# A gate and a normalisation moved from VectorE to GpSimd, w3 in quarters, and six smaller moves in a two-layer kernel

## The chip, the cores and the metric

One core of a Trainium2 chip. The metric is the device time of one execution in microseconds (us); the times of three executions and one profiled execution are given below. Engines: TensorE (PE, its weight loads PEld), VectorE (DVE), ScalarE (ACT), GpSimd (POOL), and SyncE (SP), which issues most transfers (SPq).

## What is computed

Two transformer layers over 16 sequences of 512 tokens, width 128, all in fp32. Layer 0: an attention with a running state and a gated dense network. Layer 1, cut to what matters here:

```python
x = x + attn0(norm(x)) + ffn0(norm(x))       # ffn0: ... gelu(h2 . gelu(h1 . h)) then w3
xn = layernorm(x)
# gated linear attention ("GLA"), 4 heads
gk = log_sigmoid(xn @ gk_w1 @ gk_w2 + gk_b2) / 16
o  = gated_linear_scan(xn @ Wq, xn @ Wk, xn @ Wv, gk)
o  = o / sqrt(mean(o * o) + eps) * g_norm
g  = xn @ Wg
r1 = x + (o * g * sigmoid(g)) @ Wo
# 16-head softmax attention, head width 8, then a layer norm and a routed dense network
a  = softmax(q @ k.T / sqrt(8)) @ v
y  = layernorm(xn + a @ Wo + bo)
expert = floor(y @ router_w + router_b) mod 4
out = r1 + layernorm(y + relu(y @ W1[expert] + b1) @ W2[expert] + b2)
```

## The kernel before, in words

The program has three stages, each a block in which every engine has its own list of instructions; they meet through semaphores that only count up.

**Layer 0** (`layer0_sequences`) runs a pipeline over the 16 sequences. SP also prepares weights for layer 1 there: in three of its rounds (`stage "W"`) it loads 12 chunks (L295), ScalarE and VectorE split each into a high and a low part (L443, L509), and SP stores them (L298). One buffer serves all chunks. Ahead of the load of chunk 4, SP issues 12 plain copies into the table of expert weights (`table_parts`, L292). `pad` (L300) writes 2 MB of padding rows in each round.

**Layer 1** (`attention`) is a pipeline over rounds -4 to 16; in a full round (0 to 12) each of nine stages works on another sequence. `OUT_OF` says which: F0 and F (the last product of layer 0's dense network, h2 and w3) are 4 and 3 sequences ahead, A0 (layer norm, transpose, projections of q and k) 2, A1 and B (GLA; row maxima of the scores) 1, C (softmax and product with v) 0, and C2 (output projection, norm, router, scatter) one behind. A round has 32 steps. `attention_order` writes one list of (stage, kind, number) by step with `put(step, stage, kind, number)`, and every engine walks this list in order and does its own part of each entry. In each step p TensorE makes scores p (L1305), ScalarE the exponentials (L1425); TensorE makes score rows for the maxima (L1287) and VectorE reduces them (L1578); the score rows have one pair of banks, so TensorE's maxima of step p wait for VectorE's reduction of step p-1. In odd steps TensorE multiplies with v (L1315). What else a step holds, of what is touched:

- step 12, `front`: VectorE's statistics of x1; GpSimd's `root` (L1662 adds eps, L1664 takes the power -0.5). Step 14, `front2`: VectorE's four `tensor_scalar` make xn (L1477). Step 16: TensorE transposes xn (L1194), GpSimd adds a bias row (L1676).
- step 13, `U`: VectorE makes three states from a bank of TensorE's; the second and third are updates of the one before (L1545); GpSimd then makes h_blk (L1685). Step 14, `A`: TensorE's products (L1237) take the bank of U, so they wait for the states. VectorE multiplies them with the causal mask (L1550).
- step 21: tanh of the gate on ScalarE; VectorE copies the outputs O. Step 24: `osquare` (ScalarE), `gate` (VectorE, L1516: (tanh + 1) * g), `O2` (VectorE's reduction L1559 and L1562, then GpSimd's power L1698). Step 25: `O3` (VectorE L1565, then GpSimd's product with the gate, L1702), and `rank` (TensorE). Step 26: `slot` (VectorE, L1640 to L1648, with the product L1644). Steps 24 and 26: the two halves of w3 (L1186); step 27: `x1` (VectorE adds, L1485; SP stores). Steps 28 and 29: transposes of o. Step 31: the GLA output product and the scatter.
- `warm`: in rounds -2, -1 and 13 to 15 TensorE makes five idle products (L1166) in each even step (`live`, `few`).

TensorE's first instruction of the stage waits for all dense weights (`f_loaded`, 2 MB, issued in a small block before the stage). In round -2 the first sequence is normed, transposed, projected and stored by 24 transfers (L1096), then loaded in the layout of the row maxima (L1106).

**Experts** (`experts`): VectorE first turns the counts into a plan of 19 groups of 512 tokens (L1879 to L1909), for which SP waits; then each group goes through two products; VectorE norms and `write`s it (L1945) after GpSimd's `root` (L1971, L1974), and GpSimd scatters it by four indirect transfers (L1983). GpSimd's list is root(k+1), then the scatters of k.

## Time and profile before

| | us |
|---|---|
| median of three executions | 2771.05 (2768.88 to 2776.47) |
| profiled execution, its time | 2765.3 |
| its span, first to last instruction | 2763.5 |
| layer 0 stage / layer 1 stage / experts stage, from about | 0 / 977 / 2597 |
| mean granted TensorE clock | 0.949 |

The granted clock is 1.0 at TensorE's full level and 0.5 at half. In the timeline each row has the start, the duration, the engine, the line, the operation, output and inputs, their shapes, the number of merged instructions, and in brackets how long the engine had been idle and who ended that. The views by source give the number of instructions, the least, median and greatest duration in ns, and the stretch in which they lie. In the windows each row has the stretch, its length, the busy us and instructions of PE, PEld, DVE, ACT and POOL, the mean granted clock, the DMA share and GB/s; where it is of one line alone, only the busy us and instructions of its engine.

### The profile page before, as it was taken

To read this page: it belongs to the slowest core of one execution; us is meant where nothing else is said; L and a number is where in the kernel's file an instruction comes from. 1 tells how busy PE (TensorE), PEld (TensorE's weight loads), DVE (VectorE), ACT (ScalarE), POOL (GpSimd) and SP (SyncE) were. 2 spreads that over 40 slices of the span, in tenths; PEclk is the share of its full clock that TensorE was granted. 3 is DMA by queue.
4 is the path that set the end of the run, shared out by engine and by line. 5 is a ranking of instruction groups with operands and counts; after the bars stand their busy time and mean duration, and the time that the engine had idled before them with its cause. 6 is when DMAs were issued, how large, how long until landed. Compare 5 with 4: busy or idle time off the path is not lost. (4 is left out here: it accounts for less than half of the span.)

```text
span 2763.5 us, 45274 instructions
## 1 busy us (share of the span) xinstructions
PE 2440.8 (88%) x14654; PEld 1702.0 (62%) x14654; DVE 1946.9 (70%) x3706; ACT 1345.7 (49%) x1926; POOL 591.6 (21%) x630
## 2 busy tenths in 40 slices
PE   3899999999999858889988998899888988999496
PEld 2778888888888645555555545555445545554396
DVE  3789888888888513667767777777777777672275
ACT  1444444444444312366566656666565656555142
POOL 0111112111211100111212222222222231212177
PEclk9999999999999878999999999999999999998698
DMA  5443432242232133432344323432343333301373
GB/s 153 128 124 106 130 93 74 82 136 78 74 103 80 43 138 89 119 95 75 100 127 117 89 79 114 133 91 75 100 133 100 81 102 88 85 28 37 114 236 107
DMA packets 194686, 280.31 MB, mean 101 GB/s; under 512 B 21576, under 2 KB 151065, under 8 KB 185760
## 3 DMA queue, kind: packets, MB, share of 16 engines
q1 hardware_dynamic: 189088, 266.47, 32.6%
q0 software_dynamic: 5504, 12.63, 1.3%
q8 instruction: 53, 0.87, 0.1%
q14 instruction: 41, 0.34, 0.0%
HBM read 148.65 MB, written 131.91 MB: 102 GB/s over the span
## 5 line engine op out<-in xcount | busy, mean ns | idle before, releaser
L1578 DVE TENSOR_REDUCE c_row_max<-b_psum 128x2 f32<-128x1024 f32 x512 | 624.9, 1220 | 283.6 <-PE b_psum L1287 281.0
L1425 ACT ACTIVATE c_prob<-b_psum 128x1024 f32<-128x1024 f32 x512 | 525.6, 1027 | 376.6 <-PE b_psum L1305 371.7
L1305 PE MATMUL b_psum<-c_cq,c_ck 25*128 25x512 f32 x1024 | 262.5, 508 | 76.6 <-ACT c_prob L1425 72.8
L1287 PE MATMUL b_psum<-c_bk,c_bq 24*128 24x512 f32 x1024 | 263.9, 511 | 64.2 <-DVE c_row_max L1578 54.8
L1315 PE MATMUL b_psum<-c_prob,c_v_aug 128*32 128x512 f32 x2048 | 287.0, 634 | 0.1
L1305 PEld LDWEIGHTS b_psum<-c_cq,c_ck 25*128 25x128 f32 x1024 | 96.8, 186 | 255.3 <-ACT c_prob L1425 149.2
L353 PE MATMUL a_psum<-a_yT_hi,a_w_hi 128*128 128x512 f32 x512 | 205.7, 402 | 9.1 <-issue 5.9
L353 PE MATMUL a_psum<-a_yT_hi,a_w_lo 128*128 128x512 f32 x512 | 203.2, 397 | 0.0
L353 PE MATMUL a_psum<-a_yT_lo,a_w_hi 128*128 128x512 f32 x512 | 202.8, 396 | 0.0
L1287 PEld LDWEIGHTS b_psum<-c_bk,c_bq 24*128 24x128 f32 x1024 | 97.6, 187 | 104.7 <-DVE c_row_max L1578 87.3
L459 ACT ACTIVATE a_g<-a_psum,a_cols 128x512 f32<-128x512 f32 x64 | 44.1, 690 | 238.3 <-PE a_psum L353 234.6
L517 DVE TENSOR_TENSOR_SCAN a_st_sb<-a_decay,a_kv_sb 128x512 f32<-128x512 f32 x128 | 156.7, 1225 | 4.4
L615 POOL TENSOR_TENSOR a_rs<-a_mv,a_eps 128x4 f32<-128x4 f32 x16 | 3.2, 203 | 660.6 <-DVE a_mv L540 660.6
L376 PEld LDWEIGHTS a_psum<-a_w_plain,a_outs 128*128 128x128 f32 x1024 | 135.1, 193 | 15.0 <-issue 4.0
L376 PE MATMUL a_psum<-a_w_plain,a_outs 128*128 128x128 f32 x1024 | 135.9, 276 | 3.6 <-DVE a_x L575 3.6
L1175 PE MATMUL b_psum<-c_g_hi,b_f_hi 128*128 128x512 f32 x256 | 114.3, 446 | 15.3 <-DMA c_g_lo<-g_scratch 13.2
L514 DVE SCALAR_TENSOR_TENSOR a_kv_sb<-a_psum,a_bias,a_v_sb 128x512 f32<-128x512 f32 x128 | 95.6, 747 | 44.8 <-PE a_psum L353 25.2
L1698 POOL TENSOR_TENSOR c_o_ms<-c_o_ms,b_minus_half 128x16 f32<-128x16 f32 x16 | 46.6, 2912 | 365.1 <-DVE c_o_ms L1562 365.1
L1166 PE MATMUL b_psum<-b_f_hi 128*128 128x512 f32 x400 | 119.0, 432 | 0.0
L353 PEld LDWEIGHTS a_psum<-a_yT_hi,a_w_hi 128*128 128x128 f32 x512 | 97.0, 189 | 31.6 <-issue 8.7
L447 ACT ACTIVATE a_v_sb<-a_psum,a_bias 128x512 f32<-128x512 f32 x128 | 88.8, 694 | 47.7 <-PE a_psum L353 46.8
L1662 POOL TENSOR_TENSOR c_rs<-c_mv,b_eps 128x4 f32<-128x4 f32 x32 | 6.5, 202 | 491.2 <-DVE c_mv L1471 491.2
(296 smaller groups left out, 5562.2 us busy)
## 6 DMA issues: line engine op xcount, KB each, us to landing
sorted_scratch<-a_pad SPq DMA_DIRECT2D x16, 2184.5 KB, 14.4
g_scratch<-a_g_hi SPq DMA_DIRECT2D x16, 1024.0 KB, 4.0
g_scratch<-a_g_lo SPq DMA_DIRECT2D x16, 1024.0 KB, 7.2
c_g_hi<-g_scratch SPq DMA_DIRECT2D x16, 1024.0 KB, 5.8
c_g_lo<-g_scratch SPq DMA_DIRECT2D x16, 1024.0 KB, 7.9
stack_scratch<-c_qk_hi SPq DMA_DIRECT2D x256, 64.0 KB, 1.6
d_wt<-expert_scratch SPq DMA_DIRECT2D x19, 834.0 KB, 5.6
c_bq<-stack_scratch SPq DMA_DIRECT2D x128, 96.0 KB
```

The lines of the kernel that those rows point to most:

```text
L353: mm = nc.tensor.matmul(out, a, c, start=(n == 0), stop=(n == last))
L376: mm = nc.tensor.matmul(tok[:, cut(t)], outs[:, i % OUTS, cut(t)], blk(w_plain, A_WO + i), start=(i == 0 and t == 0), stop=(i == FB0 - 1), ...
L447: nc.scalar.activation(v_sb[:, i % 2, :], bank(f"v{i}"), ACT.Identity, bias=bias[:, 4 * i:4 * i + 1]).then_inc(S["v"], 1)
L514: nc.vector.scalar_tensor_tensor(out=kv_sb[:, :], in0=bank(f"k{i}"), scalar=bias[:, 4 * i + 1:4 * i + 2], in1=v_sb[:, i % 2, :], op0=ALU.a ...
L517: nc.vector.tensor_tensor_scan(st_sb[:, :], decay[:, i:i + 1].to_broadcast([P, SEQ]), kv_sb[:, :], 0.0, ALU.mult, ALU.add).then_inc(S["sca ...
L1166: nc.tensor.matmul(psum[:, FFN[0] if add > 0 else PV, :], w_block(f_hi, n), f_hi[:, 0:BANK], start=True, stop=True)
L1175: nc.tensor.matmul(bank(f"h2{c}"), hi, g1_hi[:, k, :], start=(k == 0), stop=False)
L1287: mm = nc.tensor.matmul(psum[:, MAX + x, :], bq[r, j, cut(t)], bk[r, j, :], start=True, stop=True)
L1305: mm = nc.tensor.matmul(psum[:, SCORE + x, :], ck[r, j, cut(kb)], cq[r, j, :], start=True, stop=True)
L1315: mm = nc.tensor.matmul(psum[32 * g:32 * g + 32, PV, :], v_aug[:, kb, HPG * j + g, :], prob[:, (2 * i + g // 2) % 4, g % 2, :], start=(kb ...
L1425: nc.scalar.activation(prob[:, i % 4, :, :], psum[:, SCORE:SCORE + 2, :], ACT.Exp, scale=DH1 ** -0.5).then_inc(S["exp"], 1)
L1578: nc.vector.tensor_reduce(row_max[:, t, at:at + 3:2], psum[:, MAX:MAX + 2, :], AX.X, ALU.max).then_inc(S["row_max"], 1)
```

## The change

1. The gate goes to GpSimd as two operations, `t = t * g` and `g = t + g`; VectorE's is gone.
2. The normalisation of the next sequence goes to GpSimd, right behind `root`, as a subtraction and a product over all 512 elements; `front2` is gone.
3. w3 is made in quarters at steps 23, 25, 27 and 30; `x1` moves from step 27 to 31; `rank` and `slot` from 25 and 26 to 30 and 31; `osquare` and `gate` from 24 to 23.
4. `warm` leaves round -2. The dense weights are loaded in four parts, inside round -3 and behind g1, and TensorE waits for each part.
5. Layer 0: the 12 table copies go behind the stores of chunks 6 to 11, two each.
6. The plan of the experts is made by VectorE at the end of layer 1; TensorE makes four fp32 products of 512 columns at the start of the expert stage; GpSimd issues the scatters of group 17 ahead of root(18).

```diff
-                        if n == PREP_PER_ROUND and kind == "prep_ld":
-                            for d, plain in table_parts:
-                                sp.dma_start(d, plain).then_inc(S["table_out"], 16)
...
                             sp.dma_start(dst, prep[:, :, 0:width].bitcast(F32)).then_inc(S["prep_out"], 16)
+                            if n >= len(prep_chunks) - len(table_parts) // 2:
+                                at = 2 * (n - len(prep_chunks) + len(table_parts) // 2)
+                                for d, plain in table_parts[at:at + 2]:
+                                    sp.dma_start(d, plain).then_inc(S["table_out"], 16)
...
+W3_AT = (23, 25, 27, 30)
...
-    put(25, "C2", "rank")
-    put(26, "C2", "slot")
+    put(30, "C2", "rank")
+    put(31, "C2", "slot")
...
-    put(14, "A0", "front2")
...
-    put(24, "A1", "osquare", 0)
-    put(24, "A1", "osquare", 1)
-    put(24, "A1", "gate")
+    put(23, "A1", "osquare", 0)
+    put(23, "A1", "osquare", 1)
+    put(23, "A1", "gate")
     put(24, "A1", "O2")
-    put(24, "F", "w3", 0)
     put(25, "A1", "O3")
-    put(26, "F", "w3", 1)
-    put(27, "F", "x1")
...
+    for t, p in enumerate(W3_AT):
+        put(p, "F", "w3", t)
+    put(31, "F", "x1")
...
-            few = r in (-2, -1) or BATCH - 3 <= r < BATCH
+            few = r == -1 or BATCH - 3 <= r < BATCH
...
+            def dense_weights():
+                for c in range(HID):
+                    at = slice(HID * c * P, (HID * c + HID) * P)
+                    for part, dst in enumerate((f_hi, f_lo)):
+                        sp.dma_start(dst[:, at].bitcast(F32), d_f[:, part, at]).then_inc(f_loaded[c], 16)
...
                 if isinstance(base, int) and add == -3:
+                    dense_weights()
                     rest_of_weights()
...
                         c = i // 2
+                        if not looped and add == -3:
+                            pe.wait_ge(f_loaded[c], 32)
...
-                        for t in (2 * i, 2 * i + 1):
-                            for k in range(HID):
...
+                        for k in range(HID):
+                            mm = nc.tensor.matmul(bank("w3")[:, cut(i)], h2g[:, k, cut(i)], w_block(f_w3, k),
+                                                  start=(k == 0), stop=(k == HID - 1))
+                        if i == TILES - 1:
                             mm.then_inc(filled, 1)
...
-            pe.wait_ge(f_loaded, 32)
...
-                    elif kind == "front2":
-                        dve.wait_ge(S["xnb"], upto(stage, 1, 0))
-                        norm_scale(stage, 0, x1, xn).then_inc(S["xn"], 1)
...
-                    elif kind == "gate":
-                        dve.wait_ge(S["gate_t"], upto(stage, 1, 1))
...
             run(dve, rounds)
+            nc.vector.memset(plan_ones[:, :], 1.0).then_inc(S["plan_step"], 1)
+            dve.wait_ge(S["place"], BATCH)
...
+            nc.vector.tensor_copy(plan_i[:, :, :], plan[:, :, :]).then_inc(S["plan_i"], 1)
...
                         root(stage, 0)
+                        pool.wait_ge(S["A0_filled"], upto(stage, len(uses["A0"]), 0))
+                        mean, scale = (v.to_broadcast([P, TILES, P]) for v in (mv[:, 0, :, 0:1], rs[:, 0, 1, :].unsqueeze(2)))
+                        nc.gpsimd.tensor_tensor(xn[:, :, :], x1[:, :, :], mean, ALU.subtract).then_inc(S["xn_centred"], 1)
+                        pool.wait_ge(S["rs0"], upto(stage, 1, 1))
+                        pool.wait_ge(S["xn_centred"], upto(stage, 1, 1))
+                        nc.gpsimd.tensor_tensor(xn[:, :, :], xn[:, :, :], scale, ALU.mult).then_inc(S["xn"], 1)
...
+                    elif kind == "gate":
+                        pool.wait_ge(S["gate_t"], upto(stage, 1, 1))
+                        g = gate[:, :, :].rearrange("p t d -> p (t d)")
+                        t = e_both[:, :, :, :].rearrange("p w t d -> p (w t d)")
+                        nc.gpsimd.tensor_tensor(t, t, g, ALU.mult).then_inc(S["gate_g"], 1)
+                        pool.wait_ge(S["gate_g"], upto(stage, 1, 1))
+                        nc.gpsimd.tensor_tensor(g, t, g, ALU.add).then_inc(S["gate"], 1)
...
-            sp.wait_ge(S["plan_i"], 1)
...
+            for n in range(4):
+                nc.tensor.matmul(psum[:, Y[1], :], ident[:, :], rows[:, 0:TILES, :].rearrange("p n d -> p (n d)"), start=True, stop=True)
             turn(0)
...
-                if k + 1 < GROUPS:
+                if k + 2 < GROUPS:
                     root(k + 1)
...
+                if k + 2 == GROUPS:
+                    root(k + 1)
...
-                for part, dst in enumerate((f_hi, f_lo)):
-                    sp.dma_start(dst[:, :].bitcast(F32), d_f[:, part, :]).then_inc(f_loaded, 16)
```

## Rows read from the trace of the kernel before

**Rows 1.** The page, part 1: busy us of each engine.
```profile
PE 2440.8 (88%) x14654; PEld 1702.0 (62%) x14654; DVE 1946.9 (70%) x3706; ACT 1345.7 (49%) x1926; POOL 591.6 (21%) x630
```

**Rows 2.** Windows, two rounds of layer 0, all engines.
```profile
130.40:192.79 62.39, 57.58 (x291) 48.09 (x291) 48.32 (x88) 25.99 (x44) 8.83 (x12) 0.96 0.48 130
192.79:247.60 54.81, 54.47 (x291) 46.10 (x290) 49.15 (x88) 26.43 (x44) 9.78 (x12) 1.00 0.47 148
```

**Rows 3.** Timeline, SP's queue: first table copy, load of chunk 4.
```profile
123.17 3.76 SPq L292 DMA_DIRECT2D expert_scratch<-in_b_plain  x1
...
137.40 0.59 SPq L295 DMA_DIRECT2D a_prep_raw<-in_b_split  x1
```

**Rows 4.** Round -2: the warming products by source (ns min/median/max), and the timeline.
```profile
L1166 PE MATMUL b_psum<-b_f_hi x42: 387/393/476, 1024.5 to 1042.9; 128*128 128x512 f32 x42
...
1028.36 1.12 DVE L1477 TENSOR_SCALAR c_xn<-c_x,c_mv,c_rs 128x128 f32<-128x128 f32 x4 [1.56 <-POOL c_rs L1664]
...
1042.20 0.60 PE L1194 MATMUL b_psum<-b_ident,c_xn 128*128 128x128 f32 x4
...
1068.79 0.79 PE L1287 MATMUL b_psum<-c_bk,c_bq 24*128 24x512 f32 x2 [7.83 <-DMA c_bk<-stack_scratch]
```

**Rows 5.** Windows: twelve rounds (L1578 alone), steps 0 to 21, two tails.
```profile
1246.43:2318.53 1072.10, 468.50 (x384) 0.96 0.34 101
...
1694.18:1756.28 62.10, 57.40 (x401) 33.06 (x400) 47.11 (x95) 40.49 (x59) 15.80 (x18) 1.00 0.28 77
...
1756.28:1782.01 25.73, 21.11 (x145) 12.62 (x145) 19.04 (x23) 13.81 (x16) 5.27 (x2) 0.93 0.55 172
...
1934.23:1963.10 28.87, 23.87 (x147) 13.73 (x147) 19.03 (x23) 13.93 (x16) 5.26 (x2) 0.82 0.52 164
```

**Rows 6.** Timeline, steps 13 to 16 of the round from 1872.10 us.
```profile
1908.12 1.02 POOL L1664 TENSOR_TENSOR c_rs<-c_rs,b_minus_half 128x4 f32<-128x4 f32 x1
...
1909.38 0.29 DVE L1545 SCALAR_TENSOR_TENSOR c_states<-c_states,c_e_last,c_u_tmp 128x64 f32<-128x64 f32 x1
...
1910.00 0.28 DVE L1545 SCALAR_TENSOR_TENSOR c_states<-c_states,c_e_last,c_u_tmp 128x64 f32<-128x64 f32 x1
...
1910.34 1.05 PE L1237 MATMUL b_psum<-c_qg,c_kg 32*128 32x128 f32 x14 [0.36 <-DVE c_states L1545]
...
1914.00 1.28 POOL L1676 TENSOR_TENSOR c_xnb_o<-c_xn,b_bo_row 128x512 f32<-128x512 f32 x1 [1.01 <-DVE c_xn L1477]
```

**Rows 7.** Timeline, step 26; L1644 and L527 by source; L1644 alone.
```profile
1947.17 2.35 POOL L1702 TENSOR_TENSOR c_o_n<-c_o_n,c_gate 128x1024 f32<-128x1024 f32 x1 [1.34 <-DVE c_o_n L1565]
...
1948.42 1.14 DVE L1644 TENSOR_TENSOR c_spot<-c_spot,c_mask 128x16 f32<-128x16 f32 x1
...
L1644 DVE TENSOR_TENSOR c_spot<-c_spot,c_mask x14: 1131/1140/1147, 1322.2 to 2484.0; 128x16 f32<-128x16 f32 x14
...
L527 DVE SCALAR_TENSOR_TENSOR a_outs<-a_t_sb,a_u_sb x128: 691/693/830, 79.9 to 942.2; 128x512 f32<-128x512 f32 x128
...
2583.15 0.17 DVE L1644 TENSOR_TENSOR c_spot<-c_spot,c_mask 128x16 f32<-128x16 f32 x1
```

**Rows 8.** Timeline, steps 24 to 26 of the same round.
```profile
1942.92 2.91 POOL L1698 TENSOR_TENSOR c_o_ms<-c_o_ms,b_minus_half 128x16 f32<-128x16 f32 x1 [23.07 <-DVE c_o_ms L1562]
...
1944.65 2.05 PE L1186 MATMUL b_psum<-b_f_w,c_h2g 128*128 128x128 f32 x16
...
1945.87 1.23 DVE L1565 TENSOR_TENSOR c_o_n<-c_o_sb,c_o_ms 128x1024 f32<-128x1024 f32 x1 [1.81 <-POOL c_o_ms L1698]
```

**Rows 9.** Timeline, start of the expert stage, and the window of its start.
```profile
2599.76 0.18 DVE L1909 CAST d_plan_i<-d_plan 128x38 int32<-128x38 f32 x1
...
2608.08 0.80 PE L1831 MATMUL b_psum<-d_hT_hi,d_wt 128*128 128x512 f32 x1 [2.27 <-DMA d_wt<-expert_scratch]
...
2597.00:2614.10 17.10, 7.13 (x20) 5.60 (x21) 4.50 (x18) 3.24 (x5) 0.00 (x0) 0.50 0.69 241
```

**Rows 10.** Timeline, end of the span: the last write, behind the last root.
```profile
2745.47 1.21 DVE L1945 SCALAR_TENSOR_TENSOR d_out_sb<-d_scaled,d_rs,d_xt 128x128 f32<-128x128 f32 x4 [1.28 <-POOL d_rs L1974]
```

More of the change, by code:

```diff
@@ L975, in attention, with plan_tile @@
         slot_i = sb("slot_i", [P, TILES], I32)
+        plan_at = iter(range(0, SEQ, TILES * GROUPS + TILES))
+        def plan_tile(*shape):
+            first, n = next(plan_at), shape[0] * (shape[1] if len(shape) > 1 else 1)
+            view = qg[:, first:first + n]
+            return view if len(shape) == 1 else view.rearrange("p (a b) -> p a b", b=shape[1])
+        plan_ones, plan_number = (kg[:, GROUPS * i:GROUPS * i + GROUPS] for i in range(2))
+        plan_count, plan_groups, plan_ends, plan_jump = (kg[:, 2 * GROUPS + EXPERTS * i:2 * GROUPS + EXPERTS * (i + 1)] for i in range(4))
+        plan_over, plan_past, plan_shift = plan_tile(EXPERTS, BATCH), plan_tile(GROUPS, EXPERTS), plan_tile(GROUPS, EXPERTS)
+        plan_shift_sum = plan_tile(GROUPS)
         PV, SCORE, MAX, FFN, RING = 0, 2, 4, (1,), (6, 7)
@@ new lines, in _ @@
+            every = plan_number[:, 0:BATCH].unsqueeze(1).to_broadcast([P, EXPERTS, BATCH])
+            have = plan_count[:, :].unsqueeze(2).to_broadcast([P, EXPERTS, BATCH])
+            nc.vector.scalar_tensor_tensor(out=plan_over[:, :, :], in0=every, scalar=float(SEQ), in1=have, op0=ALU.mult,
+                                           op1=ALU.is_lt).then_inc(S["plan_step"], 1)
+            dve.wait_ge(S["plan_step"], 4)
+            nc.vector.tensor_reduce(plan_groups[:, :], plan_over[:, :, :], AX.X, ALU.add).then_inc(S["plan_step"], 1)
@@ new lines, in _ @@
+            dve.wait_ge(S["plan_step"], 11)
+            nc.vector.scalar_tensor_tensor(out=plan[:, 1, :], in0=plan_number[:, :], scalar=float(SEQ), in1=plan_shift_sum[:, :], op0=ALU.mult,
+                                           op1=ALU.add).then_inc(S["plan_step"], 1)
+            dve.wait_ge(S["plan_step"], 12)
+            nc.vector.tensor_scalar(plan[:, 0, :], plan[:, 0, :], float(EXPERTS - 1), None, ALU.min).then_inc(S["plan_step"], 1)
+            nc.vector.tensor_scalar(plan[:, 1, :], plan[:, 1, :], float(EXPERTS * CAP), None, ALU.min).then_inc(S["plan_step"], 1)
@@ L1778, in experts @@
         Y, HT, RING = (0, 1), (6, 7), (2, 3, 4, 5)
-        sems("steps", "plan_i", *(f"x_in{n}" for n in range(XB)), *(f"w_in{n}" for n in range(WB)))
+        sems(*(f"x_in{n}" for n in range(XB)), *(f"w_in{n}" for n in range(WB)))
         sems("hT", "hT_hi", "hT_lo", "w1", "hid", "y", "acc0", "acc", "stats", "mv", "rs_step", "rs", "scaled", "token", "out", *(f"out_out{n}" for n in range(OB)))
@@ L1885, in _ @@
-            have = count[:, :].unsqueeze(2).to_broadcast([P, EXPERTS, BATCH])
-            nc.vector.scalar_tensor_tensor(out=over[:, :, :], in0=step, scalar=float(SEQ), in1=have, op0=ALU.mult,
-                                           op1=ALU.is_lt).then_inc(S["steps"], 1)
-            dve.wait_ge(S["steps"], 4)
-            nc.vector.tensor_reduce(groups[:, :], over[:, :, :], AX.X, ALU.add).then_inc(S["steps"], 1)
-            dve.wait_ge(S["steps"], 5)
-            nc.vector.tensor_tensor_scan(ends[:, :], ones[:, 0:EXPERTS], groups[:, :], 0.0, ALU.mult, ALU.add).then_inc(S["steps"], 1)
@@ L1899, in _ @@
-            nc.vector.tensor_reduce(plan[:, 0, :], past[:, :, :], AX.X, ALU.add).then_inc(S["steps"], 1)
-            dve.wait_ge(S["steps"], 10)
-            nc.vector.tensor_reduce(shift_sum[:, :], shift[:, :, :], AX.X, ALU.add).then_inc(S["steps"], 1)
-            dve.wait_ge(S["steps"], 11)
-            nc.vector.scalar_tensor_tensor(out=plan[:, 1, :], in0=number[:, :], scalar=float(SEQ), in1=shift_sum[:, :], op0=ALU.mult,
-                                           op1=ALU.add).then_inc(S["steps"], 1)
@@ L2052, in layer1 @@
         place = sb("place", [P, EXPERTS])
+        plan = sb("plan", [P, 2, GROUPS])
+        plan_i = sb("plan_i", [P, 2, GROUPS], I32)
         token0 = sb("token0", [P, TILES])
```

71 lines of the change are left out of this document (26 added, 45 removed).

## The prediction

> **What bounds the kernel now.** I read four views, in this order. The page comes first: TensorE is busy for 88% of the span [rows 1], at a granted clock of 0.96 over the middle [rows 5]. So it is TensorE's own order of work, and whoever makes it wait, that sets the time. The windows by stage come next: layer 0 (its rounds are 54.4 us each, from about 78 us on) has one round that is 62.39 us where the next is 54.81 us [rows 2]. Third, the rounds of layer 1. The twelve full rounds from 1246.43 to 2318.53 us hold 384 row maxima, 32 each, so a round is 1072.10 / 12 = 89.34 us [rows 5]. The first 22 of its 32 steps took 62.10 us from 1694.18 us on and 62.13 in the round from 1872.10 us, and the variation is in the last ten, the tail: 25.73 us at a mean granted clock of 0.93, 28.87 us at 0.82 [rows 5]. Of the mean, 89.34 - 62.1 = 27.2 us, some 1.5 us over the best tail is therefore half clock. Last, the timeline of one round, at the places that the edits touch [rows 6 to 8]. VectorE is not saturated over a round, but in the tail TensorE waits for it, and in the middle for the GLA states.
>
> **Layer 0, the table copies.** SP issues twelve copies at 123.17 us, ahead of the load of chunk 4, which goes out at 137.40 us; the copies hold SP, and with it the chunk that ScalarE and VectorE split [rows 3]. The edit puts the load 14 us earlier and hangs two copies behind each of the last six stores. The stores are a step and more ahead of the next use of the buffer, so I cost the new places at nothing; if that cover were gone, each of the six could cost the 0.6 us of an issue or two. The round falls to the length of the next one: 62.39 - 54.81 = **-7.6 us** (between -9.3 and -5).
>
> **Round -2, 80 warming products fewer.** From 1024.5 to 1042.9 us TensorE ran 42 of them, at 0.23 us apart (1.3 us for five, the record's 0.39 us overlaps), before and just behind the transpose of the first sequence. That transpose came at 1042.20 us, though its input was ready at 1028.36 + 1.12 = 1029.5 us [rows 4]. Behind it hangs a strict chain: projections, 24 stores of 0.47 us, loads, and the first row maximum at 1068.79 us [rows 4]. Without the 40 warming products ahead of it the transpose is 9.3 us earlier, less the three waits of some 1.1 us for the single bank of the dense product that they now fill: **-6.1 us** (between -8 and, should the clock fall there, -2). GpSimd's normalisation has xn ready at about 1031 us, before the transpose even so. The dense weights now come in four parts behind g1, on the same queue and in the same amount; TensorE needs one part and g1, 2.5 MB, from a start 5 us later, where it now waits for all 4 MB. I take 0 (between -2 and +2).
>
> **Middle of each round: the normalisation goes to GpSimd.** VectorE loses four instructions at step 14, 1.12 us by the same four in round -2 [rows 4]. Step 15 is TensorE's, without a gap, so this frees nothing. GpSimd gains two passes over 512 elements, 1.28 us each by its nearest operation, right behind the power that ends at 1909.14 us [rows 6]. They are late for nobody by themselves: xn is ready near 1911.9 us, the transpose runs at 1916. But VectorE's two state updates, at 1909.38 and 1910.00 us, each read two SBUF tensors, and fall inside these passes [rows 6]. What happens then is seen in the tail: a 16-element product of two SBUF tensors takes 0.17 us when GpSimd rests, and 1.13 to 1.15 us in all 14 cases in which GpSimd's 2.35 us product runs; it ends with it, at 1948.42 + 1.14 = 1949.56 against 1947.17 + 2.35 = 1949.52 us [rows 7]. So the first update ends at about 1910.45, the second behind the second pass, at about 1909.1 + 1.28 + 0.2 + 1.05 to 1.28 = 1911.7 us, instead of 1910.29: **+1.4 us** (between +0.7, if VectorE gets in first once, and +1.65). TensorE's products A wait for exactly these states (the 0.36 us idle [rows 6]), and so does VectorE's next maximum, behind which stands TensorE's. The full delay stays, since all of step 15 follows in TensorE's order. Its idle time there grows from 0.4 to 1.8 us, just ahead of TensorE-bound work. In the tail such gaps ended in half clock; a low stretch of 3.4 us over busy work costs up to 1.7 us. I put half of that on the middle: **+0.8 us** (0 to 1.6).
>
> The page "SBUF — State Buffer" of the Trainium skill (section "SBUF: two separate sides") has a rule that speaks against this move: VectorE with two SBUF inputs and GpSimd share one pair of ports, whoever starts first holds it for the whole instruction, and the other blocks. The rows on the product agree; for the state updates, by that rule, the price would be the same 1.4 us, and with no such lock it would be 0.
>
> **Tail of each round.** VectorE loses the gate (priced like O3, 1.23 us [rows 8], which has as many elements), the slot (5 small operations, one of them 1.14 us long by the same hold) and x1 (0.68 us) between steps 24 and 28. TensorE's 4 us of w3 (two halves of 2.05 us [rows 8]) goes from steps 24 and 26 to 23, 25, 27 and 30. GpSimd makes the gate in 2 x 2.35 = 4.7 us from 1934.0 us on, done at 1938.9, ahead of its power at 1942.92 us [rows 7, 8]; no operation of VectorE with two SBUF inputs lies there. What stays is the chain O2 (1.2 us), power (2.91 us), O3 (1.23 us), in which VectorE already idles 1.81 us [rows 8]. Followed step by step with these durations, from the score of step 22 at 0: reduction 24 at 4.6, O2 5.8, power 7.25 to 10.2, O3 10.2, reduction 26 at 11.4, reduction 27 at 13.2, score 28 at 15.05 us, where it is now 15.2. Step 28 falls from 2.9 to 1.65 us (no slot, no x1 ahead of its maximum), but step 30 rises from 1.7 to 2.45, with a quarter of w3 (1.03 us) and rank (0.55 us) in it. At full clock the tail is 25.2 instead of 25.7 us: **-0.5 us** (-1.2 to 0). Step 27 to 31 have hardly a gap left, so half clock should fall more on stretches where TensorE waits anyway: of the 1.5 us I give back **-0.7 us** (-1.5 to 0). x1 and the slot at step 31 delay the first maxima of the next round: **+0.1 us** (0 to 0.6). SP's store of x1 is 12 us later and so are the loads behind it, which are due 16 steps on: nothing.
>
> **Rounds, summed.** 1.4 + 0.8 - 0.5 - 0.7 + 0.1 = +1.1 us, thirteen times +14.3. Rounds -1 and 13 have the hold too, +2.8; rounds 13 and 14 are relieved of gate and slot, -2. Together **+15.1 us**.
>
> **Experts.** The plan leaves the start: today 2597.0 to 2599.94 us, with SP, and so the first weights at 2608.08 us, behind it [rows 9]. That is -2.9. Four fp32 products of 512 columns, 1 to 2 us each, end by about 2604 us, before the weights at 2605.2, and let the first group run at full clock; until 2614 us it now runs at half, some 6 us of work of which 2.1 come back: -5.0 us in all (-6 to -2). At the end GpSimd issues the scatters of group 17 ahead of the last root. VectorE waits 1.28 us for that root today, ahead of the last write [rows 10]; the root then also queues behind the scatters, and an equal piece is added: +1.3 us. Together **-3.7 us**.
>
> **Sum.** -7.6 - 6.1 + 0 + 15.1 - 3.7 = -2.3 us. The profiled execution took 2765.3 us (span 2763.5), 5.7 us under the median 2771.05; -2.3 puts the changed kernel at 2763 in such an execution and at a median of **2769 us**.
>
> **Rivals.** (1) *Slower: the hold brings the half clock every round.* The longer gap in front of step 15 costs 1.6 us, and the tail gives back only its 0.5: 1.4 + 1.6 - 0.5 + 0.1 = 2.6 a round, 34 + 0.8 - 17.4 = +17 us, 2788 us. For it speaks that gaps of 1 to 2 us in the tail do end in low clock; against it that the middle is densely busy on both sides. It decides from about 1.9 us a round. (2) *No hold on the state updates.* Then a round changes by -0.5 - 0.7 + 0.1 = -1.1 us: -14.3 - 2 - 17.4 = -34 us, 2737 us. The held product is a tensor_tensor, the updates are scalar_tensor_tensor; but layer 0's of that kind, with two SBUF inputs, stretches from 0.69 to as much as 0.83 us [rows 7], in places where a pass of GpSimd runs into it. (3) *The tail gains more.* The half clock of the tail goes entirely and the middle stays at full clock: 1.4 - 0.5 - 1.5 + 0.1 = -0.5 a round, so -6.5 + 0.8 - 17.4 = -23 us, 2748 us. For it: best tails of 25.7 us exist today.
>
> **How the numbers follow.** The forecast, 2761 to 2779 us, gets 0.42; rival 1 gets 0.25, rival 2 gets 0.12, rival 3 with what lies between it and the forecast 0.21. A measurement of this kernel tells about 0.3%, 8.3 us, from no change: below 2762.7 lie rivals 2 and 3 and a little of the forecast, 0.35; above 2779.4 lies rival 1, 0.26; between them 0.39. The range reaches to 2746 (most of rival 3) and 2787 (most of rival 1).
>
> **What would show it.** After: both state updates of step 13 long (0.8 us and more) or late, and the products A with over 1.5 us idle behind them; the normal round above 89.3 us, its first 22 steps at 63.5 to 64.3, its last ten near 26; the layer 0 round from 130 us at 55 us; the first row maximum some 14 us earlier than 1068.79; 11 us between the start of the expert stage and its first product cut to about 8. The prediction is wrong if the updates keep their 0.28 us, or if the granted clock in the middle or the tail moves by more than I allowed.

## The result and the profile after

The changed kernel takes a median of 2810.63 us in four executions (2788.27 to 2822.53), the kernel before 2771.94 us in four (2768.88 to 2776.47). The ratio is 1.0124, 95% interval 1.0085 to 1.0162: slower by 1.2%, where I had forecast no difference, and above the range of 2746 to 2787 us. The profiled execution took 2788.27 us (span 2786.2, mean granted clock 0.935); the other three had spans of 2801.7 to 2820.4 us at 0.916 to 0.925.

The two spans, cut at the same places (first scan of layer 0's last round, first row maximum on VectorE, first score of rounds 0 and 13, last score, last scatter of layer 1, end), in us:

| stretch | before | after | difference | predicted |
|---|---|---|---|---|
| layer 0, to its last round | 900.5 | 898.0 | -2.5 | -7.6 |
| to the first row maximum | 169.1 | 157.5 | -11.6 | -6.1 |
| round -1, to the first score | 89.5 | 91.1 | +1.6 | +1.4 |
| rounds 0 to 12 | 1159.4 | 1198.3 | +38.9 | +14.3 |
| rounds 13 to 15, to the last score | 243.9 | 240.6 | -3.3 | -0.6 |
| last steps of layer 1 | 26.1 | 26.6 | +0.5 | 0 |
| switch of stage, experts, to the end | 175.0 | 174.1 | -0.9 | -3.7 |
| sum | 2763.5 | 2786.2 | +22.7 | -2.3 |

So the loss is all in the full rounds. The windows of the changed kernel, to be read against [rows 5]: rounds 1 to 12 (L1589, which is now the row maximum, alone), then steps 13 to 16 of two rounds, then a tail.

```profile
1240.30:2344.96 1104.66, 468.50 (x384) 0.92 0.34 98
...
1455.39:1467.88 12.49, 10.38 (x105) 6.15 (x105) 11.04 (x25) 5.11 (x7) 7.30 (x8) 1.00 0.13 39
1636.76:1652.06 15.30, 13.32 (x104) 7.93 (x104) 11.03 (x25) 5.16 (x7) 7.30 (x8) 0.78 0.24 66
1668.95:1694.90 25.95, 22.32 (x145) 12.14 (x144) 16.34 (x21) 13.75 (x16) 9.87 (x4) 0.87 0.42 136
```

A round is 1104.66 / 12 = 92.06 us, where it was 89.34. Steps 13 to 16 took 11.3 us in every full round before. Now they take 12.5 to 12.6 us at a clock of 1.00 in three rounds of thirteen, and 15.1 to 16.5 us with stretches at half clock in the other ten. In the second row shown these are the same 104 or 105 products, TensorE busy for 13.32 us instead of 10.38. The timeline of step 13, against [rows 6] (L1556 are VectorE's two state updates, L1718 and L1721 GpSimd's two passes of the normalisation, L1257 the products A):

```profile
1915.97 1.05 POOL L1718 TENSOR_TENSOR c_xn<-c_x,c_mv 128x512 f32<-128x512 f32 x1
1916.25 0.85 DVE L1556 SCALAR_TENSOR_TENSOR c_states<-c_states,c_e_last,c_u_tmp 128x64 f32<-128x64 f32 x1
...
1917.02 0.27 DVE L1553 TENSOR_SCALAR c_u_tmp<-b_psum,c_e_both 128x64 f32<-128x64 f32 x1
1917.16 1.04 POOL L1721 TENSOR_TENSOR c_xn<-c_xn,c_rs 128x512 f32<-128x512 f32 x1
1917.42 0.85 DVE L1556 SCALAR_TENSOR_TENSOR c_states<-c_states,c_e_last,c_u_tmp 128x64 f32<-128x64 f32 x1
...
1918.33 0.82 PE L1257 MATMUL b_psum<-c_qg,c_kg 32*128 32x128 f32 x10 [1.50 <-DVE c_states L1556]
```

Both updates take 0.85 us instead of 0.28, and each ends with the pass of GpSimd that it overlaps: 1916.25 + 0.85 = 1917.10 beside 1915.97 + 1.05 = 1917.02, and 1918.27 beside 1918.20. TensorE is idle 1.50 us ahead of A, where it was 0.36. The hold is as forecast and so is its price, 12.48 - 11.31 = 1.17 us; the half clock behind it was not. In the ten rounds the clock falls 0.3 to 2.3 us behind the start of A.

The tail takes 25.95 us in the round shown, at a mean clock of 0.87. GpSimd's gate takes two passes of 2.37 us and is done 2.58 us ahead of its power (against [rows 8]):

```profile
1942.09 2.37 POOL L1749 TENSOR_TENSOR c_e_both<-c_e_both,c_gate 128x1024 f32<-128x1024 f32 x1 [14.23 <-ACT c_e_both L1384]
1944.53 2.37 POOL L1751 TENSOR_TENSOR c_gate<-c_e_both,c_gate 128x1024 f32<-128x1024 f32 x1
1949.48 2.91 POOL L1754 TENSOR_TENSOR c_o_ms<-c_o_ms,b_minus_half 128x16 f32<-128x16 f32 x1 [2.58 <-DVE c_o_ms L1573]
```

Layer 0, the windows of the two rounds that answer to [rows 2]:

```profile
130.10:186.00 55.90, 55.56 (x291) 46.99 (x291) 48.69 (x87) 26.04 (x44) 8.99 (x12) 0.98 0.37 116
186.00:245.10 59.10, 55.24 (x291) 46.02 (x290) 49.06 (x87) 26.39 (x44) 8.86 (x12) 1.00 0.51 157
```

And the timeline of SP and VectorE around the second of them, against [rows 3]:

```profile
180.74 6.06 SPq L292 DMA_DIRECT2D a_prep_raw<-in_b_split  x1
...
195.11 0.69 DVE L510 TENSOR_TENSOR a_prep<-a_prep_raw,a_prep 128x512 fp32r<-128x512 f32 x1 [4.98 <-ACT a_prep L444]
```

The first of them is relieved, 62.39 to 55.90 us. The other has grown from 54.81 to 59.10: the load of chunk 8 now holds SP for 6.06 us behind four of the copies and the padding (3.71 us before), and VectorE stands idle for 4.98 us over that chunk (1.90 us before).

Round -2, against [rows 4]: without warming products the transpose of the first sequence runs at 1029.67 us and not at 1042.20, and the first row maximum at 1054.74 instead of 1068.79.

```profile
1029.67 0.60 PE L1214 MATMUL b_psum<-b_ident,c_xn 128*128 128x128 f32 x4
...
1054.74 0.79 PE L1307 MATMUL b_psum<-c_bk,c_bq 24*128 24x512 f32 x2 [12.64 <-DMA c_bk<-stack_scratch]
```

The expert stage, timeline of its start and of its end, against [rows 9] and [rows 10]:

```profile
2620.85 5.20 PE L1889 MATMUL b_psum<-b_rows,b_ident 128*128 128x512 f32 x8 [14.39 <-PEq L893]
2621.82 0.39 SPq L1838 DMA_DIRECT2D d_xt<-sorted_scratch  x1
...
2629.09 0.50 PE L1874 MATMUL b_psum<-d_hT_hi,d_wt 128*128 128x512 f32 x1 [2.60 <-DMA d_wt<-expert_scratch]
...
2768.87 0.98 POOL L1996 DMA_INDIRECT out<-d_out_sb,d_token  x1 [0.30 <-issue]
...
2770.17 1.04 POOL L1987 TENSOR_TENSOR d_rs<-d_rs,b_minus_half 128x4 f32<-128x4 f32 x1
2771.32 1.14 DVE L1958 SCALAR_TENSOR_TENSOR d_out_sb<-d_scaled,d_rs,d_xt 128x128 f32<-128x128 f32 x4 [7.26 <-POOL d_rs L1987]
```

The first load goes out 0.97 us into the stage, the first product comes 8.24 us into it (11.08 before), and the four fp32 products last 5.20 us. The first group's first product takes 0.50 us where it took 0.80. At the end the last root stands behind eight scatters in a row, and VectorE idles 7.26 us ahead of the last write.

### The profile page after: what moved, and what is told of

Its sections match the earlier page's. It is cut to its first block and busy times, and to the rows that moved or that the text cites. A ratio compares the mean times of both kernels' runs of the same rounds, so it can differ in the third digit from the quotient of the medians.

```text
span 2786.2 us, 45143 instructions
## 1 busy us (share of the span) xinstructions
PE 2463.2 (88%) x14582; PEld 1696.1 (61%) x14582; DVE 1927.0 (69%) x3626; ACT 1344.1 (48%) x1926; POOL 701.2 (25%) x694
## 5 line engine op out<-in xcount | busy, mean ns | idle before, releaser
L1589 DVE TENSOR_REDUCE c_row_max<-b_psum 128x2 f32<-128x1024 f32 x512 | 624.8, 1220 | 350.7 <-PE b_psum L1307 347.2
L1307 PE MATMUL b_psum<-c_bk,c_bq 24*128 24x512 f32 x1024 | 270.7, 524 | 49.5 <-DVE c_row_max L1589 35.6
L1335 PE MATMUL b_psum<-c_prob,c_v_aug 128*32 128x512 f32 x2048 | 305.8, 672 | 0.1
L377 PEld LDWEIGHTS a_psum<-a_w_plain,a_outs 128*128 128x128 f32 x1024 | 134.2, 192 | 12.8 <-issue 1.7
L1196 PE MATMUL b_psum<-c_g_hi,b_f_hi 128*128 128x512 f32 x256 | 120.1, 469 | 18.2 <-DMA b_f_lo<-f_split_scratch 11.3
L1206 PEld LDWEIGHTS b_psum<-b_f_w,c_h2g 128*128 128x128 f32 x512 | 81.6, 244 | 55.7 <-issue 47.0
L1375 ACT COPY c_h2g<-b_psum 128x512 f32<-128x512 f32 x64 | 37.5, 587 | 154.6 <-PE b_psum L1198 152.9
```

The lines of the kernel that those rows point to most:

```text
L377: mm = nc.tensor.matmul(tok[:, cut(t)], outs[:, i % OUTS, cut(t)], blk(w_plain, A_WO + i), start=(i == 0 and t == 0), stop=(i == FB0 - 1), ...
L1196: nc.tensor.matmul(bank(f"h2{c}"), hi, g1_hi[:, k, :], start=(k == 0), stop=False)
L1206: mm = nc.tensor.matmul(bank("w3")[:, cut(i)], h2g[:, k, cut(i)], w_block(f_w3, k), start=(k == 0), stop=(k == HID - 1))
L1307: mm = nc.tensor.matmul(psum[:, MAX + x, :], bq[r, j, cut(t)], bk[r, j, :], start=True, stop=True)
L1335: mm = nc.tensor.matmul(psum[32 * g:32 * g + 32, PV, :], v_aug[:, kb, HPG * j + g, :], prob[:, (2 * i + g // 2) % 4, g % 2, :], start=(kb ...
L1589: nc.vector.tensor_reduce(row_max[:, t, at:at + 3:2], psum[:, MAX:MAX + 2, :], AX.X, ALU.max).then_inc(S["row_max"], 1)
```

## The experiments

All of them also ran beside the kernel before on the same chip; the ratios are to it. That kernel's own median was 2758.73 us beside the runs whose names begin with a_norm and b_, 2766.40 beside those with n_ and 2765.15 beside the other three, so a difference of a few us between kernels of different groups is read from the stretches of the profiles and not from the medians. The first table has the mean over rounds 0 to 12 of the profiled execution, in us, cut at the starts of the scores, with the time at half clock inside each part in brackets.

| kernel | steps 0-12 | 13-16 | 17-21 | 22-31 | round |
|---|---|---|---|---|---|
| before | 33.82 | 11.31 (0) | 16.88 (0) | 27.17 (7.1) | 89.18 |
| after | 33.94 | 14.90 (6.0) | 17.14 (0.6) | 26.19 (8.7) | 92.18 |
| a_norm_back | 34.05 | 11.31 (0) | 16.89 (0) | 26.63 (10.8) | 88.86 |
| a_norm_late | 33.93 | 11.34 (0) | 16.89 (0) | 26.71 (11.3) | 88.87 |
| b_norm_only | 34.05 | 14.71 (5.8) | 17.01 (0.3) | 28.03 (9.7) | 93.80 |
| b_gap | 33.94 | 14.81 (5.0) | 16.90 (0) | 28.18 (8.9) | 93.83 |
| a_gap_filled | 33.93 | 10.77 (0) | 19.43 (3.7) | 26.44 (10.0) | 90.57 |
| n_gate_back | 33.93 | 11.31 (0) | 16.89 (0) | 26.51 (7.9) | 88.64 |
| n_tail_back | 34.16 | 11.31 (0) | 16.89 (0) | 26.47 (8.1) | 88.83 |
| best_w3 | 33.82 | 11.30 (0) | 16.89 (0) | 26.40 (12.9) | 88.42 |
| best_fill | 33.94 | 11.44 (0.3) | 19.99 (5.8) | 26.38 (12.9) | 91.75 |

| kernel | median, us | ratio to before, 95% interval |
|---|---|---|
| a_norm_back | 2737.84 | 0.9920 (0.9895 to 0.9944) |
| a_norm_late | 2738.43 | 0.9918 (0.9892 to 0.9943) |
| b_norm_only | 2818.33 | 1.0209 (1.0183 to 1.0234) |
| b_gap | 2831.48 | 1.0261 (1.0231 to 1.0292) |
| a_gap_filled | 2769.34 | 1.0007 (0.9989 to 1.0025) |
| n_gate_back | 2740.34 | 0.9907 (0.9885 to 0.9929) |
| n_tail_back | 2738.24 | 0.9893 (0.9869 to 0.9916) |
| n_warm_nodummy | 2746.29 | 0.9927 (0.9905 to 0.9949) |
| n_root_copies | 2732.23 | 0.9876 (0.9854 to 0.9898) |
| best_w3 | 2729.51 | 0.9879 (0.9848 to 0.9909) |
| best_fill | 2772.28 | 1.0036 (1.0021 to 1.0050) |

**Which part loses: a_norm_back.** The changed kernel with the normalisation back on VectorE.

```diff
+    put(14, "A0", "front2")
...
+                    elif kind == "front2":
+                        dve.wait_ge(S["xnb"], upto(stage, 1, 0))
+                        norm_scale(stage, 0, x1, xn).then_inc(S["xn"], 1)
...
-                        nc.gpsimd.tensor_tensor(xn[:, :, :], x1[:, :, :], mean, ALU.subtract).then_inc(S["xn_centred"], 1)
...
-                        nc.gpsimd.tensor_tensor(xn[:, :, :], xn[:, :, :], scale, ALU.mult).then_inc(S["xn"], 1)
```

> The changed kernel with one thing undone: VectorE makes xn again by its four tensor_scalar in step 14, and GpSimd's subtraction and product are gone. Theory (the hold): the two state updates of step 13 go back from 0.85 us to 0.28 us, TensorE's idle time ahead of the products A from 1.50 to some 0.36 us, and the half clock that follows it in steps 15 and 16 of ten of thirteen rounds goes too. Steps 13 to 16 take 11.3 us (before: 11.3; changed: 12.5 at full clock, 15.1 to 16.3 with half clock), a round 88.0 us, the span some 2732 us, the median 2735 to 2745. Rival (the middle lost its clock for another reason, the gate on GpSimd or the quarters of w3): only the 1.2 us of a round come back, the half clock of the middle stays, and the median stays above 2780.

2737.84 us. Steps 13 to 16 of the round from 1590.92 us, in the windows:

```profile
1624.85:1636.16 11.31, 10.35 (x104) 6.21 (x104) 10.80 (x29) 5.08 (x7) 5.30 (x6) 1.00 0.08 22
```

Every full round has its 11.3 us back, at a clock of 1.00. This one part carried the whole loss; all the others together make the kernel 0.8% faster.

**Engine or moment: a_norm_late.** The same two passes on GpSimd, one step down its list.

```diff
+    put(14, "A0", "norm")
...
                         root(stage, 0)
+                    elif kind == "norm":
                         pool.wait_ge(S["A0_filled"], upto(stage, len(uses["A0"]), 0))
```

> The changed kernel, with GpSimd's subtraction and product moved one step down its list, behind the product that makes h_blk out of the states: the same work on the same engine, but it starts when the state updates are over. Theory (the hold of the updates is the whole cause): as with the normalisation on VectorE, steps 13 to 16 in 11.3 us and no half clock there; xn is ready some 3 us later, near the transpose that needs it, which may cost up to 1 us a round; median 2735 to 2755. Rival (GpSimd's two passes cost wherever they stand, by their own activity or by memory traffic): the middle stays at 12.5 us and more and the median above 2780.

2738.43 us, the same as with VectorE. The timeline of steps 13 to 15:

```profile
1630.26 0.28 DVE L1557 SCALAR_TENSOR_TENSOR c_states<-c_states,c_e_last,c_u_tmp 128x64 f32<-128x64 f32 x1
...
1631.21 1.05 PE L1258 MATMUL b_psum<-c_qg,c_kg 32*128 32x128 f32 x14 [0.36 <-DVE c_states L1557]
...
1633.81 1.04 POOL L1720 TENSOR_TENSOR c_xn<-c_x,c_mv 128x512 f32<-128x512 f32 x1
...
1634.99 1.04 POOL L1723 TENSOR_TENSOR c_xn<-c_xn,c_rs 128x512 f32<-128x512 f32 x1
1635.00 1.29 DVE L1562 TENSOR_TENSOR c_a_sb<-b_psum,b_causal 128x512 f32<-128x512 f32 x2 [0.18 <-PE b_psum L1258]
```

The updates are at 0.28 us, TensorE's idle time at 0.36. The second pass now runs beside two of VectorE's mask products, which read one bank and one SBUF tensor and keep the 1.29 us of the kernel before. So it was not the work on GpSimd, but the moment at which it stood beside two operations with two SBUF inputs.

**The part alone: b_norm_only.** The kernel before with GpSimd's normalisation and nothing else of the change.

```diff
-    put(14, "A0", "front2")
...
+                        nc.gpsimd.tensor_tensor(xn[:, :, :], x1[:, :, :], mean, ALU.subtract).then_inc(S["xn_centred"], 1)
...
+                        nc.gpsimd.tensor_tensor(xn[:, :, :], xn[:, :, :], scale, ALU.mult).then_inc(S["xn"], 1)
```

> The kernel before, with one part of the change alone: GpSimd makes xn by a subtraction and a product behind root, VectorE's four instructions are gone. Theory: this part alone brings the loss. Both updates 0.85 us, TensorE idle 1.5 us ahead of A, steps 13 to 16 in 12.5 us at full clock and 15 to 16 us where the clock falls; 1.2 to 4.5 us a round, median 2787 to 2830. Rival (it takes the lighter tail or the gate on GpSimd for the clock to fall in the middle): only the 1.2 us, 2786 us at most, with no low stretch near step 15.

2818.33 us, 59.6 over the kernel before on that chip. In 8 of 13 rounds steps 13 to 16 hold half clock, up to this:

```profile
1662.55:1678.96 16.41, 14.69 (x104) 8.79 (x105) 11.01 (x25) 5.16 (x7) 7.29 (x8) 0.69 0.28 77
```

It takes neither the lighter tail nor the gate; the rival is out. The tail grew as well, 27.17 to 28.03 us, with 9.7 us at half clock instead of 7.1.

**Is it the gap or GpSimd: b_gap.** VectorE's own normalisation, ahead of the states. No hold and no new work anywhere, only later states.

```diff
+    put(13, "A0", "front2")
     put(13, "A1", "U")
...
-    put(14, "A0", "front2")
```

> The kernel before, with VectorE's own four tensor_scalar of the normalisation moved from step 14 to step 13, ahead of the states. GpSimd does nothing new and holds nothing; the states are late by some 1.2 to 1.4 us all the same, by VectorE's own work. Theory (the half clock follows TensorE's longer idle time, whoever makes it): the same picture as with the normalisation on GpSimd, low stretches near step 15 or 16 in most rounds, median 2787 to 2830. Rival (the half clock comes from GpSimd's activity and not from the idle time): 1.3 us a round, 17 us in all, and no low stretch in the middle: some 2788 us.

2831.48 us, 72.8 over the kernel before. The timeline of step 13 of the round from 1630.79 us:

```profile
1667.93 1.11 DVE L1477 TENSOR_SCALAR c_xn<-c_x,c_mv,c_rs 128x128 f32<-128x128 f32 x4 [0.37 <-POOL c_rs L1664]
...
1670.18 0.28 DVE L1545 SCALAR_TENSOR_TENSOR c_states<-c_states,c_e_last,c_u_tmp 128x64 f32<-128x64 f32 x1
...
1670.52 0.71 PE L1237 MATMUL b_psum<-c_qg,c_kg 32*128 32x128 f32 x8 [1.84 <-DVE c_states L1545]
```

And the window of steps 13 to 16 of the same round, one without half clock:

```profile
1664.71:1677.51 12.80, 10.36 (x104) 6.16 (x104) 10.99 (x29) 5.08 (x7) 5.24 (x6) 1.00 0.13 41
```

The updates keep 0.28 us, TensorE is idle 1.84 us ahead of A, a round without half clock takes 12.8 us there and seven rounds of thirteen take 15.8 to 17.0. So VectorE alone makes the same loss: the half clock follows TensorE's idle time, whoever causes it.

**The gap filled, the hold kept: a_gap_filled.** A half of h2 moves into the wait for the states.

```diff
-H2_AT = (2, 6, 7, 10, 13, 15, 17, 19)
+H2_AT = (2, 6, 7, 10, 13, 13, 17, 19)
```

> The changed kernel, normalisation on GpSimd as it stands, with one edit: a half of h2 (6 products, 1.4 us of TensorE) goes from step 15 to the end of step 13, into the time in which TensorE waits for the states. The hold of the updates by GpSimd stays. Theory (what costs is TensorE's idle time ahead of A, its 1.2 us and the half clock behind it): the updates stay at 0.85 us, the idle time falls from 1.50 us to 0.1 to 0.4 us, steps 13 to 16 take 11.3 to 11.6 us, no half clock in the middle; median 2735 to 2750. Rival (the long updates or GpSimd's passes lower the clock or slow the round by themselves): median above 2780.

2769.34 us: level with the kernel before, where the changed one was 1.2% above it, and not the 2735 to 2750 that I expected; the rival's 2780 and more did not come either. The windows of steps 13 to 16 and 17 to 21 of one round:

```profile
1631.49:1642.22 10.73, 10.09 (x104) 6.36 (x104) 10.11 (x25) 5.04 (x6) 7.29 (x8) 1.00 0.01 4
1642.22:1661.51 19.29, 18.12 (x109) 10.69 (x108) 13.09 (x29) 13.22 (x18) 0.86 (x2) 0.91 0.45 115
```

And the timeline of steps 13 to 17 of another:

```profile
1909.12 0.85 DVE L1556 SCALAR_TENSOR_TENSOR c_states<-c_states,c_e_last,c_u_tmp 128x64 f32<-128x64 f32 x1
...
1910.03 0.97 PEld L1257 LDWEIGHTS b_psum<-c_qg,c_kg 32*128 32x128 f32 x16 [0.42 <-DVE c_states L1556]
...
1914.73 0.63 PE L1214 MATMUL b_psum<-b_ident,c_xn 128*128 128x128 f32 x4 [0.54 <-DVE c_a_sb L1561]
...
1916.37 0.79 PE L1307 MATMUL b_psum<-c_bk,c_bq 24*128 24x512 f32 x2 [0.58 <-DVE c_row_max L1589]
```

The updates are still held at 0.85 us, the weight load of A waits 0.42 us and its products hardly at all (the maximum ahead of them ends 0.1 us before), and steps 13 to 16 are faster than ever, at full clock. But step 15 lacks the h2 that covered VectorE's mask products: two new gaps of 0.54 and 0.58 us open in steps 16 and 17, and half clock comes behind them: steps 17 to 21 go from 16.9 to 19.4 us. The theory holds for its place; the cover was taken from another.

**The tail: n_gate_back and n_tail_back**, both on top of a_norm_back. One returns the gate to VectorE (in step 23), the other the quarters, rank, slot and x1 to their old steps:

```diff
-W3_AT = (23, 25, 27, 30)
+W3_AT = (24, 24, 26, 26)
...
-    put(30, "C2", "rank")
-    put(31, "C2", "slot")
+    put(25, "C2", "rank")
+    put(26, "C2", "slot")
...
-    put(31, "F", "x1")
+    put(27, "F", "x1")
```

> The version with the normalisation back on VectorE (median 2737.8 us, span 2735.7), and the gate back on VectorE too, as one operation in step 23. Theory (the last ten steps are set by TensorE's order and the chain of O2, power and O3, and the gate on GpSimd lies beside it for nothing): VectorE's 1.22 us in step 23 sit ahead of its maximum of that step, so up to 1.2 us a round come back, or nothing if VectorE has that much idle time there; the last ten steps at 26.6 to 27.8 us, median 2738 to 2753. Rival (the gate on GpSimd costs something too, by holding VectorE's operations with two SBUF inputs): faster than 2735 us.

> The version with the normalisation back on VectorE, and w3, x1, rank and slot back in the steps of the kernel before (24 and 26, 27, 25, 26); gate and osquare stay in step 23 and on GpSimd. Theory (the quarters and the later slot and x1 give the 0.5 us a round at full clock that I predicted): the last ten steps 0.3 to 1.0 us longer, 4 to 13 us in all, median 2742 to 2751. Rival (the whole gain of the last ten steps comes from the gate, and the quarters give nothing): within 3 us of 2738.

2740.34 and 2738.24 us. Neither edit can be told from a_norm_back: the tail is 26.5 to 26.6 us in all three. With the steps as before it goes from 24.5 to 29.8 us from round to round; with the change's steps, in a_norm_back, from 25.9 to 27.0. The expected 0.3 to 1.0 us for the quarters is not there; a_norm_back holds 10.8 us of half clock in its tail and n_tail_back 8.1, so a gain at full clock may hide behind it, which no run shows. Both edits together were not undone, and `osquare` stays in step 23 in all three: what brought the tail from 27.2 us to these 26.5 stays open.

**Layer 0 and the end: n_root_copies**, on top of a_norm_back, with the last root ahead of the scatters again and the copies in the last full round of layer 0.

```diff
-                            if n >= len(prep_chunks) - len(table_parts) // 2:
...
+                        if isinstance(base, int) and add == BATCH - 1:
+                            for d, plain in table_parts:
+                                sp.dma_start(d, plain).then_inc(S["table_out"], 16)
...
-                if k + 2 < GROUPS:
+                if k + 1 < GROUPS:
                     root(k + 1)
...
-                if k + 2 == GROUPS:
-                    root(k + 1)
```

> The version with the normalisation back on VectorE, with two places of the change made otherwise: GpSimd's last root ahead of the scatters of group 17, as in the kernel before, and the twelve table copies issued at the end of layer 0 (its round 15), not behind the stores of chunks 6 to 11. Theory: the last write of the experts is not 7 us late, the time from the write of group 17 to the end 24.6 us where it is 26.5, -1.9 us; no round of layer 0 above 55 us (they are 54.6 and 59.7 now), -5 us. Median 2731. Rival for the copies (the round from 186 us is long because of chunk 8's load behind the 2 MB padding, whatever the copies): that round stays at 59 to 60 us, median 2736.

2732.23 us. Layer 0's round that starts near 186 us falls from 59.7 to 56.1 us (to 54.8 in best_w3 and best_fill, which have the same copies; in all seven with the copies behind the stores it is 59.1 to 60.6). Its last round starts at 893.6 us, 5.4 us earlier than in a_norm_back and 6.9 earlier than in the kernel before, but 2.6 of the 5.4 lie ahead of the first scan, at 74.9 us and not 77.6, where the two kernels are the same. The last write waits 1.28 us for its root instead of 7.26, and from the write of group 17 to the end it is 24.6 us, where a_norm_back has 26.5:

```profile
2712.10 1.21 DVE L1955 SCALAR_TENSOR_TENSOR d_out_sb<-d_scaled,d_rs,d_xt 128x128 f32<-128x128 f32 x4 [1.28 <-POOL d_rs L1984]
```

**Warming and fp32 products: n_warm_nodummy**, on top of a_norm_back.

```diff
-            few = r == -1 or BATCH - 3 <= r < BATCH
+            few = r in (-2, -1) or BATCH - 3 <= r < BATCH
...
-            for n in range(4):
-                nc.tensor.matmul(psum[:, Y[1], :], ident[:, :], rows[:, 0:TILES, :].rearrange("p n d -> p (n d)"), start=True, stop=True)
```

> The version with the normalisation back on VectorE, with two parts undone: TensorE's warming products are back in round -2, and the four fp32 products at the start of the expert stage are gone. Theory: the first row maximum comes 6 to 11 us later, measured from the last scan of layer 0 (158 us in the version that it starts from, 169 us in the kernel before); without the four products the first group runs at half clock and the first write comes 15.4 us behind the first product where it is 13.9, +1.5 us. Median 2746 to 2750. Rival (the earlier start of layer 1 comes from loading the dense weights in parts, not from the warming products): the 158 us stay, median 2739.

2746.29 us. The first row maximum comes 166.1 us behind the last round of layer 0 (a_norm_back 158.4): 7.7 us for the warming products. The transpose runs at 1038.15 us, 139.5 us behind that round's start where a_norm_back has 132.8:

```profile
1038.15 0.60 PE L1215 MATMUL b_psum<-b_ident,c_xn 128*128 128x128 f32 x4
```

The first write of the experts comes 15.1 us behind the first product and not 13.9, so the four fp32 products are worth 1.1 us here.

**A better tail: best_w3 and best_fill**, on top of n_root_copies.

```diff
-W3_AT = (23, 25, 27, 30)
+W3_AT = (24, 26, 27, 30)
```

> The fastest version so far (normalisation on VectorE, last root ahead of the scatters, table copies late; median 2732.2, span 2730.2), with the quarters of w3 at steps 24, 26, 27 and 30 instead of 23, 25, 27 and 30. Step 24 and 26 are the ones in which TensorE waits for ScalarE's exponentials (1.16 and 1.19 us idle, with no product with v and no quarter of w3 in them). Theory: the quarters fill these gaps, the last ten steps fall from 26.6 to 24.5 to 25.5 us, and less half clock follows; median 2712 to 2724. Rival (the chain of O2, power and O3 sets the tail whatever TensorE does meanwhile): within 4 us of 2732.

> The version with the quarters of w3 at steps 24, 26, 27 and 30, with the half of h2 at the end of step 13 instead of 15 as well. With the states in time, TensorE's idle time ahead of A is 0.3 us, so the half of h2 fills little there and makes the score of step 14 1.4 us later for ScalarE. Theory: steps 13 to 16 unchanged within 0.4 us a round, so within 5 us of the version without it. Rival (the small gap in the middle still counts): 5 us faster or more.

best_w3 took 2729.51 us, the least of all and not the 2712 to 2724 that I expected; its interval overlaps that of n_root_copies. The tail stayed at 26.4 us, with 12.9 us of half clock a round instead of 11.3. In its one round with 6.8 us of half clock the tail took 24.6 us, where n_root_copies' took 25.95 with as much: so the quarters may fill the gaps and the clock take it back, but one round does not show that. best_fill, with the half of h2 moved as above, took 2772.28 us, where I had expected it within 5 us of best_w3: steps 17 to 21 at 20.0 us, half clock there in 12 of 13 rounds. It has no held update, so the half clock of these steps, in a_gap_filled too, does not need the hold. With no gap to fill, moving the cover away only costs.

## Why the prediction was wrong, step by step

**The step that failed** is the half clock of the middle, the term "+0.8 us (0 to 1.6)". The gap of 1.50 us ahead of A brought half clock in 10 of 13 rounds of the profiled execution. Steps 13 to 16 rose by 14.90 - 11.31 = 3.6 us a round, of which 1.17 are the gap and 2.4 the clock (6.0 us at half clock in a mean round); steps 17 to 21 lost another 0.26. That is rival 1, which I gave 0.25, and more than its 1.6 us. I had bounded the term by a single low stretch of 3.4 us and halved it. My own rows spoke against that bound: the tail of 28.87 us at a mean clock of 0.82 holds 2 x 0.18 x 28.87 = 10.4 us at half clock, and the mean tail of the kernel before holds 7.1. The middle has 6.8 us in most such rounds and up to 13.7, and loses some 0.4 us for each of them. Rival 1's 2788 us is what the profiled execution took, but that is luck: the median, which it was meant for, is 23 us above. The first 22 steps took 66.0 us a round, where I had named 63.5 to 64.3 as the sign of my forecast. b_norm_only and b_gap show that the gap alone is enough, a_gap_filled that the hold without the gap is harmless in its own steps. The Trainium skill's page "TensorE: Matmul & The Clock Gate" (section "Part 1: The HAM clock gate") says that the clock is set by how busy TensorE has been; these runs agree: the eight profiles with at most 0.62 us idle ahead of A have no half clock in steps 13 to 16, the three with 1.5 us and more have it in 7 to 10 of 13 rounds.

**The hold** was right in place, mechanism and size: +1.4 us forecast, 1.17 measured, both updates ending with GpSimd's passes. The passes took 1.05 us each and not the 1.28 that I took from the nearest row. This is the rule cited from the Trainium skill's page "SBUF — State Buffer"; rival 2 (no hold) is out, and the counterpart in a_norm_late agrees with the same rule: operations with one SBUF input were not held. But one case in the kernel before goes against the rule. In the expert stage 35 of VectorE's operations with two SBUF inputs start while GpSimd's power on 4 elements runs. By the rule they would be held, and they keep 0.34 to 0.35 us each:

```profile
2642.23 1.14 DVE L1936 SCALAR_TENSOR_TENSOR d_scaled<-d_acc,d_mv,b_rows 128x128 f32<-128x128 f32 x4
...
2642.72 1.04 POOL L1974 TENSOR_TENSOR d_rs<-d_rs,b_minus_half 128x4 f32<-128x4 f32 x1
```

So what holds in these runs are the passes over 512 and 1024 elements; why the power does not was not tested.

**The tail.** -0.5 - 0.7 + 0.1 = -1.1 us forecast, 26.19 - 27.17 = -1.0 measured. The size is right, but by luck: half clock there rose from 7.1 to 8.7 us a round, where I had it falling, and neither the gate's nor the quarters' share can be told from nothing. The -0.5 "at full clock" started from a tail of 25.7 us that was itself at a mean clock of 0.93. How much shorter the work at full clock got is not shown: from round to round the tail grows by 0.36 us for each us at half clock in the kernel before, and by 0.15 in the changed one. Rival 3 is out.

**Layer 0.** -7.6 forecast, -2.5 measured. The failing step is "I cost the new places at nothing". The cover named there was the next use of the buffer; what the copies delayed was the load of chunk 8, which follows them on SP behind the padding. Its round rose by 4.3 us, and the copies moved away give back 3.6 (n_root_copies) to 4.9 us (best_w3) of the 59.7 in a_norm_back. The other round fell by 6.5 us.

**Round -2 and the weights.** -6.1 + 0 forecast, -11.6 measured. The warming products were worth 7.7 us, near my lower bound of -8; I had set three waits of 1.1 us against the saving, and most of that did not come. TensorE's first product came 2.2 us earlier against the last round of layer 0 (94.7 us behind it, 96.9 before), just outside the -2 to +2 of the weights in parts. The remaining 1.7 us is within what this stretch varies by: in the nine profiles without the warming products it is 157.5 to 160.1 us, in those of the kernel before, b_norm_only and b_gap 165.1 to 169.1.

**Experts.** The plan's -2.9 was 2.8. The first write comes 13.55 us behind the first product where it was 15.39: -1.8 against -2.1. The root's order cost 1.9 where I had 1.3: the root stands behind eight scatters. Another 1.6 us or so between the first and the eighteenth write is in this execution alone (117.1 us, in the other profiles 115.2 to 115.5). Rounds 13 to 15 gained 3.3 us where I had 0.6; they held 37.5 us of half clock before and 27.3 after, and 10.2 to 44.4 in the other profiles, and the cause was not tested.

**Between executions.** The other three are 15.6 to 34.3 us longer than the profiled one, at a lower clock. From 0.935 to 0.917 the time at half clock, 2 x (1 - clock) x span, rises from 362 to 468 us and the span by 34.2 us, 0.32 us for each; that fits half clock in still more rounds, but where it lies there was not seen. It is also why the median is 39 us over the kernel before's, and the profiled execution only 23 over its profiled one. a_norm_back, without the gap, spreads over 1.7 us.

## What to carry to other kernels

When work moves to GpSimd, look at which VectorE operations with two SBUF inputs stand beside it, and who waits for them; one step later in the list made it free here. An added wait of a microsecond in a stretch where TensorE is nearly saturated is not priced at its length: here it cost three times that, its own 1.17 us and 2.4 more through the clock. And before filling a gap with work from elsewhere, ask what that work covered where it stood.
